# Attention stage of a four-stage image network: the convolution's steps cut into six pieces instead of nine

## What is computed

```python
y = relu(conv3x3(ln(x), entry_w) * entry_s + entry_b)       # 256 -> 128 channels
qv, qh = relu(y @ vqk_w * ...), relu(y @ hqk_w * ...)       # 16 channels each
A_v = softmax(qv . qv along a column)                       # "down"
A_h = softmax(qh . qh along a row)                          # "along"
feat = relu(y @ val_w * val_s + val_b)
s_v = A_v @ feat
x_v = s_v * gate(mean over a row of s_v)                    # six small layers: x @ w0, 4 hidden, x @ we
s_h = A_h @ x_v
x_h = s_h * gate(mean over a column of s_h)                 # the same kind of six layers
x = x + concat(relu(x_h @ end_w * ...), relu(mean(x) @ il_w * ...))
```

## Time and profile before

| | us |
|---|---|
| median of 3 runs (1117.77 to 1118.6) | 1118.08 |
| the profiled execution | 1117.34 |
| its span, from first to last instruction | 1115.3 |
| pass 1, from its first convolution step to that of pass 2 | 26.71 |
| pass 2 | 29.64 |
| pass 3 | 28.60 |
| pass 4 | 29.70 |
| pass 5 | 30.44 |
| pass 6 | 27.52 |

### The profile page before, as it was taken

How to read it: one execution, slowest core, us unless ns; L and a number is a source line. 1 busy time by engine, 2 the same in 40 slices (tenths; PEclk the granted TensorE clock), 3 DMA queues, 4 the chain that set the end, 5 groups by cost and what they waited for, 6 DMA issues and landing times. The chain is left out here.

```text
span 1115.3 us, 19881 instructions
## 1 busy us (share of the span) xinstructions
PE 960.4 (86%) x5702; PEld 797.9 (72%) x5702; DVE 617.2 (55%) x1714; ACT 521.8 (47%) x1336; POOL 268.2 (24%) x274
## 2 busy tenths in 40 slices
PE   6866579999999999995568898998755799998999
PEld 2743368888888888885345666676544699997998
DVE  6887643232332323322856677766888355555776
ACT  6527354343443434443234433433335466667774
POOL 0000022121221212102773200000000445443775
PEclk9558659999999999998689999999555799999999
DMA  9544401111111111113743111112230344443655
GB/s 384 246 152 151 151 29 48 58 52 53 53 52 58 49 56 53 52 42 111 230 141 95 57 39 39 38 39 76 86 141 1 123 136 140 138 133 116 191 155 150
DMA packets 63236, 114.72 MB, mean 103 GB/s; under 512 B 9698, under 2 KB 43124, under 8 KB 62132
## 3 DMA queue, kind: packets, MB, share of 16 engines
q1 hardware_dynamic: 49908, 77.74, 19.8%
q0 software_dynamic: 12960, 35.41, 11.0%
q10 hardware_dynamic: 288, 0.47, 0.1%
HBM read 73.98 MB, written 39.59 MB: 102 GB/s over the span
## 5 line engine op out<-in xcount | busy, mean ns | idle before, releaser
L601 POOL DMA_INDIRECT experts_rows_sb<-h_rows,choices x142 | 134.3, 946 | 711.5 <-POOLq L429 382.9
L796 DVE TENSOR_TENSOR experts_a_sb<-experts_a_sb,experts_bankU 128x512 f32<-128x512 f32 x71 | 48.9, 689 | 225.3 <-PE experts_bankU L184 225.3
L747 ACT ACTIVATE experts_a_sb<-experts_bankG 128x512 f32<-128x512 f32 (+1 forms) x142 | 69.6, 490 | 92.5 <-PE experts_bankG L184 92.4
L738 ACT ACTIVATE experts_hT<-experts_bankH 128x256 fp32r<-128x256 f32 x142 | 54.2, 382 | 90.5 <-PE experts_bankH L664 90.4
L760 ACT ACTIVATE experts_y_sb<-experts_bankY 128x256 f32<-128x256 f32 x142 | 54.6, 384 | 86.9 <-PE experts_bankY L181 66.8
L1185 POOL DMA_INDIRECT attn_y<-y_rows,choices x64 | 64.9, 1015 | 90.4 <-POOLq L121 38.2
L182 PE MATMUL attn_bankC<-attn_padded,attn_w_high 128*128 128x512 f32 x144 | 68.1, 473 | 18.1 <-ACT attn_feat L1471 15.9
L917 POOL DMA_INDIRECT shared_y<-y_rows,choices x64 | 68.8, 1074 | 38.4 <-POOLq L556 19.2
L181 PE MATMUL experts_bankY<-down_plain,experts_aT_plain 128*128 x284 | 72.9, 379 | 0.0
L187 DVE TENSOR_TENSOR experts_aT<-experts_bankA,experts_aT 128x256 fp32r<-128x256 f32 x142 | 59.6, 420 | 22.9 <-ACT experts_aT L755 22.9
L671 PE MATMUL experts_bankA<-konst_sb,experts_a_sb 128*128 128x128 f32 x426 | 69.9, 273 | 1.7 <-DVE experts_aT L187 1.7
(11 more groups left out here) (368 smaller groups left out, 2723.3 us busy)
## 6 DMA issues: line engine op xcount, KB each, us to landing
y_rows<-experts_y_sb SPq DMA_DIRECT2D x142, 128.0 KB, 1.7
h_rows<-xn SPq DMA_DIRECT2D x32, 256.0 KB, 2.1
mix_xT<-in_xt SPq DMA_DIRECT2D x4, 1024.0 KB, 12.2
x_res<-in_x SPq DMA_DIRECT2D x4, 1024.0 KB, 14.1
gate_raw<-in_L_ffn_gate_w SPq DMA_DIRECT2D x2, 2048.0 KB, 12.9
up_raw<-in_L_ffn_up_w SPq DMA_DIRECT2D x1, 4096.0 KB, 24.7
x_rows<-x_res SPq DMA_DIRECT2D x16, 256.0 KB, 2.5
x_res<-x_rows SPq DMA_DIRECT2D x8, 512.0 KB, 4.6
```

Of the source, the lines that this page charges most:

```text
L601: nc.gpsimd.indirect_dma_start(rows[t % DEPTH][:, :], None, h_dram, bass.IndirectOffsetOnAxis(ap=ids_i[:, t:t + 1], axis=0)).then_inc(s_ro ...
L747: nc.scalar.activation(a_sb[i % RING][:, :], bankG[i % RING][:, 0:hidden], ACT.Silu if gate is not None else ACT.Relu).then_inc(s["act"], 1)
L796: nc.vector.tensor_tensor(a_sb[i % RING][:, :], a_sb[i % RING][:, :], bankU[i % RING][:, 0:hidden], ALU.mult).then_inc(s["a"], 1)
```

## The change

Only the list of calls in the TensorE loop is rewritten. The 18 steps are cut into six pieces of three instead of nine of two; the first gap holds gate layers 0 and 1, and every later layer stands in the gap in which the one after it stood, up to layer 5. `turn(i+1, 0)` stands behind step 12 instead of step 8, gate layer 5 behind step 15 instead of step 12, and no convolution is left between `turn_gated` and `attend_along`. No instruction is added or taken away.

```diff
                     finish(i - 4)
-                    convolve(i, 0, 2)
+                    convolve(i, 0, 3)
                     gate_layer(i - 2, 0)
                     project_queries(i - 1)
                     project_values(i - 1)
-                    convolve(i, 2, 4)
+                    gate_layer(i - 2, 1)
+                    convolve(i, 3, 6)
                     turn_rows(i - 5, 0)
-                    gate_layer(i - 2, 1)
-                    convolve(i, 4, 6)
+                    gate_layer(i - 2, 2)
+                    convolve(i, 6, 9)
                     turn_rows(i - 5, 1)
-                    gate_layer(i - 2, 2)
                     scores(i - 1)
-                    convolve(i, 6, 8)
+                    gate_layer(i - 2, 3)
+                    convolve(i, 9, 12)
                     turn(i + 1, 0)
-                    gate_layer(i - 2, 3)
-                    convolve(i, 8, 10)
+                    route(i - 5)
                     gate_layer(i - 2, 4)
-                    convolve(i, 10, 12)
-                    route(i - 5)
+                    convolve(i, 12, 15)
                     branch(i)
                     gate_layer(i - 2, 5)
-                    convolve(i, 12, 14)
                     turn(i + 1, 1)
                     turn_probs(i - 1, "down")
                     turn_logits(i - 5)
                     turn_probs(i - 1, "along")
-                    convolve(i, 14, 16)
+                    convolve(i, 15, 18)
                     turn_gated(i - 2)
                     attend_down(i - 1)
-                    convolve(i, 16, 18)
                     attend_along(i - 2)
```

## The result

The changed kernel took **1134.48 us** (median of 5 runs, 1132.31 to 1137.82) against 1117.77 us for the kernel before (5 runs, 1116.19 to 1118.60): a ratio of **1.0156**, 95% interval 1.0140 to 1.0173. It is slower; the forecast was 1134. The profiled execution took 1132.31 us with a span of 1130.2 us, 14.9 us more than the span before. Every line number behind `turn` is lower by 3 than in the rows of before (`relu` L1468 for L1471).

A forecast was written before the change was run, and what follows sets the result against it. A ring over TensorE, VectorE and ScalarE was taken to bound the kernel. Passes 1 to 5 +10.7, pass 6 -0.4, pass 7 +1.0, clock +5 make +16.3 us on 1117.34: 1133.6, plus the median's 0.74, said as 1134; range 1126 to 1141.

The forecast's parts named there:

- ring of TensorE, VectorE and ScalarE: Chain through turn, last `leaky`, `turn_probs`, `deviations`, `normalise` and `relu` sets the pass; passes 1 to 5 together +10.7 us.
- pauses at gate layer 5: TensorE's wait at gate layer 5 or the branch: 2 to 2.6 us in passes 2 to 5.
- Steps ahead of the turn: Four more steps and gate layer 3 before `turn(i+1, 0)`: 3.1 us later in pass 1, 3.3 in every pass after.
- The waits of `copy_down`: Its waits for TensorE before the probabilities are saved: 5.7 us at most over passes 2 to 5, 2.9 at least.
- Passes 6 and 7: Pass 6: -0.4 us from fewer switches on TensorE; pass 7: +1.0 us, since `attend_down` stands behind all 18 steps.
- The stretch behind pass 7: Passes 8 to 10, without convolution, have gate layers in another order: 0, within -0.5 and +1 us.
- The clock: Longer TensorE pauses bring low-clock stretches, three new ones at starts of passes 3 to 6: +5 us, bounds 0 and +10.
- The 8.5 us for TensorE from gate layer 5 to the next pass: TensorE's own work from last `leaky` to next pass: some 8.5 us, while the ring needs 10.55.
- TensorE as the limit: Rival: way from turn to `relu` has slack, so fewer cuts and covered `feat` waits give 9 us, 1109; chance 0.08.
- Every pause at the low clock: Rival: pauses at pass starts and gate layer 5 all cost clock: +22 us, 1140; chance 0.16.
- The ring without the clock: Rival: pauses end without a loss of clock: +11.3 us, 1129; chance 0.20.
- That it cancels out: Rival: the longer stretch before the turn is paid back by the waits that go: 1118; chance 0.06.

The follow-up runs named there:

- e1: Changed kernel with `turn(i+1, 0)` moved back from behind step 12 to behind step 9: 1120.20 us, ratio 1.0021 to the kernel before.
- e2: Kernel before with only `turn(i+1, 0)` moved from behind step 8 to behind step 12: 1147.64 us, ratio 1.0265.
- e3: Changed kernel with zero-weight products filling TensorE's pauses (before the branch and gate layer 5, passes 2 to 5; before `turn_probs`, pass 1): 1132.47 us.
- e10: Kernel before with `relu`, `copy_feat2` ahead of `normalise`, sums behind `copy_attended`, VectorE's `normalise_rows`, `join`, low halves and SyncE's row stores later: 1107.71 us.

## Why the prediction was right

*The bound.* The ring of TensorE, VectorE and ScalarE was read from three timelines of one pass, and e1 and e2 bear it out from both sides: the turn back, 14.3 us gone; the turn late and nothing else changed, some 30 us lost. The pauses at gate layer 5 came to 2.50, 2.50, 2.58 and 2.00 us in passes 2 to 5, where 2 to 2.6 were forecast.

*Steps ahead of the turn* (3.1 in pass 1, 3.3 behind). Measured from the first step to the turn, the shift was +3.14, +2.16, +4.87, +3.53 and +2.97 us in passes 1 to 5. The price of a step was right. Pass 2 had a low stretch at its start before, and has none now; pass 3 had none and now has one. Passes 2 and 4 have their turn 14.23 us behind the first step, pass 3 has it at 15.59: that stretch cost 1.36 us, where 1.4 was put down.

*The waits of `copy_down`* (0, -1.0, -1.5, -2.3, -0.8). From the turn to the next pass the change was -0.02, -0.16, +0.18, -2.30 and -1.16. Passes 1, 4 and 5 are near what was predicted. In passes 2 and 3 the saving was lost. In pass 3 `copy_down` still waited 1.42 us, since the branch, gate layer 5, the turn and `turn_probs` ran at the low clock, and e3, without that, got 1.75 us back. In pass 2 that wait did go, but behind `copy_down` the pass took 9.39 us where it took 8.43 before: the nine products ahead of `turn_gated` took 3.34 us (623.72 to 627.06), mostly at the low clock (2.41 in pass 5, at 1.00), so `copy_gated` and with it `normalise` came 1.0 us late, as the lines of pass 2 above show. In e3, without a low stretch there, that way is 8.42 again. "From `copy_down` to `relu` VectorE and ScalarE have no slack and do the same work" left out this second way into `normalise`; only the rival of 1140 had it, at 0.9 in each of four passes.

*Passes 6 and 7* (-0.4, +1.0) came to -0.22 and +1.30. The stretch behind pass 7, put at 0 with +1 as its bound, came to +1.2.

*The clock* (+5) had the right sign and the wrong place. It was put at the starts of passes 3 to 6, behind pauses of 2 us, and taken as costing little behind gate layer 5, where TensorE was to have 2 us to spare. In fact only pass 3 began low, and the other stretches fell behind `turn_probs` and gate layer 5. The step that failed is that one on the spare time at the end of a pass. The 8.5 us for TensorE from gate layer 5 to the next pass hold at the full clock: they were 8.8 in pass 5 (718.64 to 729.17 less the pause of 1.75). With a low stretch they were 9.8 in pass 4 and 11.3 in pass 3 (653.77 to 665.99 less the pause of 0.90), and in passes 2 and 3 products of the ring itself stood in that stretch. So the pauses at the starts of passes 4 and 5 came to 0.90 and 0.95 and not to 2 each; those of passes 3 and 6 came to 2.83 and 1.75. The net of the clock was nearer 3 us: 1.36 and 1.75 in pass 3, 1.0 in pass 2, less 1.1 for the stretch that pass 2 no longer has (3.3 less 2.16). With 11.3 for the ring, that is 14.3, what the seven passes lost.

*Luck.* That the median was met within half a microsecond is in part luck. The sum of 16.3 us was made for the profiled execution, and that one lost 15.0 (1117.34 to 1132.31). The changed kernel's profiled execution lies 2.17 us under its median, where 0.74 was added; the two errors, of 1.3 and 1.4 us, cancel.

*The rivals.* TensorE as the limit (1109) is refuted by the wait for `feat`, as long as before. The prediction said that its own ring would be open if that wait shrank; it didn't. Every pause at the low clock (1140) is refuted by passes 5 and 6, which kept 1.00 behind pauses of 2.00 and 1.75 us. The ring without the clock (1129) fell short by the 3 us above; those are read from the traces, since the medians of e3 and of the changed kernel don't tell it apart. That it cancels out (1118) is refuted by the time.

## What to carry to other kernels

Before products are gathered into longer runs on TensorE, look for the one product that another engine's chain starts from: here its place counted, and the number of groups hardly did. Moving it by three steps (behind step 12 and not 9) cost 14 us, and gathering the rest cost 2 or nothing. When the tail of such a ring is cut, read at once what stands next behind it. Here the cut of `relu` showed the sums, and the cut of the sums showed VectorE's other work and a load that SyncE had queued behind a store, each only when the cut was made. And a pause that is filled can come back elsewhere: in e3 TensorE stood still at the start of the next pass in place of gate layer 5.

## What the runs showed of the hardware

The same length of pause did not always have the same consequence. Behind pauses of 2.50 to 2.58 us at gate layer 5 the granted clock fell to 0.50 in passes 2, 3 and 4 of the changed kernel, for 3.4 to 6.8 us; behind one of 2.00 in pass 5 it stayed at 1.00. And a low stretch need not cost anything: filling the pause of pass 1 in e3 took it away there, and the pass took 29.79 us for 29.83. It costs where products of the ring lie in it: 1.0 us in pass 2 and 1.75 in pass 3 of the changed kernel. Nor was a long pause always needed: pass 4 of e3 had pauses of 0.48, 0.35 and 0.16 us from gate layer 5 to the probabilities and a low stretch behind them. Executions of one and the same kernel differ as well: those of e10 lie between 1102.26 us at a mean granted clock of 0.897 and 1110.71 us at 0.889. That the clock makes the whole difference wasn't shown.
